# Seven tiles of one field's rows fetched by SyncE, and the first chunk numbers worked out on all partitions

## The chip, the cores and the metric

One core of a Trainium2 chip runs the kernel. The metric is the device time in microseconds. The kernel before took 483.76 us (median of three runs, 483.4 to 483.77).

## The reference

2048 samples have 13 dense features and 26 sparse fields. Each field has its own table of 12500 rows of 32 floats. The sparse numbers go up to 99998; a number past the end of its table reads the last row, and a negative one counts from the end, so the kernel clamps and wraps them.

```
emb = stack(table[f][sparse[:, f]])                  # 2048 x 26 x 32
bi  = emb[:, FIRST] * emb[:, SECOND]                 # 325 pairs of fields
a   = relu(bi @ att_w_w + att_w_b)                   # 32 -> 8
w   = softmax(a @ att_d_w + att_d_b over the pairs)
out = sigmoid(concat(sum(w * bi), dense) @ fin_w + fin_b)
```

## The kernel before, in words

The samples are 16 tiles of 128, taken in four blocks of four tiles (`QUADS`, the loop variable `q`). In a block the 26 fields are taken in order. For field `f`, `emb[:, f]` is a 128x128 tile: four tiles of samples (index `g` or `t = 4q + g`) with 32 numbers each.

How the rows get there depends on the field. For 23 fields GpSimd gathers them, one indirect DMA for each tile (line 368), so 92 in each block and 368 in all. It gathers a block's field as soon as VectorE has transposed the same field of the block before. For fields 3, 11 and 19 (`LOOK`) TensorE picks them: each table is in SBUF as 128 partitions x 7 chunks x 14 rows, VectorE makes one-hot columns from the chunk number of every sample (`make_onehots`, line 667, in two parts of 4 and 3 chunks), TensorE multiplies them with the table (`look_up`, line 391), and VectorE masks the right one of 14 rows and sums (lines 678, 681). This takes 12 tiles of two steps in each block, set between the other work by `STEP_FIELDS`. The steps of a block for field 3 stand in the block before; those of the first block stand at the very start, ahead of anything else on TensorE.

The chunk numbers go a long way. `look_index` comes in as 48x128, VectorE works out the chunk numbers on 48 partitions (lines 593 to 605), ACT's queue writes them to DRAM (`chunk_numbers`, line 495) and waits, and then reads the first block's back broadcast to all 128 partitions (line 498). SyncE does this for the later blocks into two buffers (`load_chunks`, line 337); for block `q` of 2 or more it first waits until the one-hots of block `q-2` are made. The same queue loads the three tables of 1568 KB (`load_table`, line 331): table 0 at once, table 1 after the first chunk numbers have landed, and table 2 after six transposes.

VectorE then transposes each field (lines 655, 657) and multiplies it with all fields before it into a ring of 8 groups of 16 pairs (line 691). TensorE multiplies each group with the attention weights (`first`, 405) and with the final weights (`sums_f`, 415), ACT applies the relu (507), TensorE sums the scores (429), and they go back transposed for the softmax. At the end of each block come maximum, exponentials and weighted sums (lines 717 to 772). Each engine's program is a fixed order written out by hand, joined by semaphores. SyncE has nothing to issue from its last `load_chunks` until it stores the result.

Of the kernel before, what the change touches and what calls it, by code (L numbers as in the profile page):

```python
# [5 lines left out]
P = 128  # L6
G = 4
# [8 lines left out]
HIDDEN = 6  # L16
BATCH = 4
LOOK = (3, 11, 19)
LOOK_TILES = (4, 4, 4)
CHUNKS = 7  # L20
CHUNK_ROWS = 14
# [16 lines left out]

def attention_fm(nc, dense, sparse, tables, params, look_index, chunk_numbers, out):
    f32, i32 = mybir.dt.float32, mybir.dt.int32  # L40
# [74 lines left out]
    def gathers_of(f):  # L115

        if f in LOOK:
            return G - LOOK_TILES[LOOK.index(f)]
        return G

# [47 lines left out]
    with ctx:  # L168
        def sb(name, shape, dt=f32):
            return ctx.enter_context(nc.sbuf_tensor(name, shape, dt))  # L170
# [4 lines left out]
        def sem(name):  # L175
# [6 lines left out]
        rows = sb("rows", [P, T, F], i32)  # L182
        emb = sb("emb", [P, F, G * D])

        look_table = sb("look_table", [P, LOOKS, CHUNKS, CHUNK_ROWS * D])

        index = sb("index", [QUADS * LOOKS * G, P], i32)
        index_clamped = sb("index_clamped", [QUADS * LOOKS * G, P])
        index_wrap = sb("index_wrap", [QUADS * LOOKS * G, P])
        index_part = sb("index_part", [QUADS * LOOKS * G, P])  # L190
        index_chunk = sb("index_chunk", [QUADS * LOOKS * G, P])
# [18 lines left out]
        wrap, moved = (weighed[:].rearrange("p g e -> p (g e)")[:, i * T * F:(i + 1) * T * F].rearrange(  # L210
            "p (t f) -> p t f", f=F) for i in range(2))
        neg_max = sb("neg_max", [P, G])
        neg_max_early = sb("neg_max_early", [P, G])
# [9 lines left out]
        feats = sb("feats", [P, T, N_DENSE])  # L223
        feats_w = sb("feats_w", [P, T, N_DENSE])
        linear = sb("linear", [P, T])
# [24 lines left out]
        rows_first_ready = sem("rows_first_ready")  # L250
        rows_ready = sem("rows_ready")
        gathered = [sem(f"gathered{f}") for f in range(F)]
        transposed = sem("transposed")
        look_table_in = [sem(f"look_table_in{n}") for n in range(len(LOOK))]
        index_in = sem("index_in")
        index_steps = sem("index_steps")
# [60 lines left out]

        def chunk_numbers_of(q):
            return chunk_numbers[q:q + 1].broadcast_to((P, LOOKS * G * P))

        block = ctx.enter_context(nc.Block())

        @block.sync
        def _(sp):
            sp.dma_start(ids[:], sparse.rearrange("(p t) f -> p t f", t=T)).then_inc(ids_in, 16)
            sp.dma_start(index[:], look_index).then_inc(index_in, 16)
            stacked = tables.rearrange("f v d -> (f v) d")

            def load_table(n):
                rows_n = stacked[LOOK[n] * V:LOOK[n] * V + P * PART_ROWS]  # L330
                sp.dma_start(look_table[:, n], rows_n.rearrange("(p c i) d -> p c (i d)", p=P, c=CHUNKS)
                             ).then_inc(look_table_in[n], 16)
# [8 lines left out]
            sp.dma_start(feats[:], dense.rearrange("(p t) n -> p t n", t=T)).then_inc(feats_in, 16)  # L341
# [12 lines left out]
        def _(pool):  # L354
            stacked = tables.rearrange("f v d -> (f v) d")
            pool.wait_ge(rows_first_ready, 1)
            for q in range(QUADS):
                for f in range(F):
                    if q == 0 and f == FIRST_FIELDS:
                        pool.wait_ge(rows_ready, 1)  # L360
                    if q and gathers_of(f):
                        pool.wait_ge(transposed, (q - 1) * F + f + 1)
                    for g in range(gathers_of(f)):
                        if q == 0 and f < FIRST_FIELDS:
                            row = rows_first[:, g, f:f + 1]
                        else:
                            row = rows[:, q * G + g, f:f + 1]
                        pool.indirect_dma_start(  # L368
                            emb[:, f, g * D:(g + 1) * D], None, stacked, bass.IndirectOffsetOnAxis(ap=row, axis=0),
                        ).then_inc(gathered[f], 16)  # L370

        @block.tensor
        def _(pe):
# [5 lines left out]
            for q in range(QUADS):  # L379

                def look_up(i):
                    of, n, g, part = steps[i]
                    pe.wait_ge(look_table_in[n], 16)
                    pe.wait_ge(onehot_made, (of * LOOKS + n) * len(STEPS) + part + 1)
# [104 lines left out]
        def _(act):  # L489
            act.dma_start(par[:, cols["offset"]], params[:, cols["offset"]]).then_inc(offsets_in, 16)  # L490
            rest = slice(cols["offset"].stop, params.shape[1])
            act.dma_start(par[:, rest], params[:, rest]).then_inc(par_in, 16)

            act.wait_ge(index_chunk_made, 1)
# [3 lines left out]
            act.dma_start(chunk_of[:, 0].rearrange("p n b -> p (n b)"), chunk_numbers_of(0)).then_inc(chunk_of_in[0], 16)  # L498
            act.wait_ge(par_in, 16)
            for q in range(QUADS):  # L500
# [71 lines left out]
        def _(dve):  # L572
# [4 lines left out]
            def make_rows(made, t, f, to, ready):  # L577
# [12 lines left out]


            dve.wait_ge(index_in, 16)
            nc.vector.tensor_scalar(index_clamped[:], index[:], float(-V), float(V - 1), ALU.max, ALU.min
# [19 lines left out]
            for n, f in enumerate(LOOK):  # L613
# [12 lines left out]
                                               look_id[:, n, :], ALU.mult, ALU.add).then_inc(look_id_steps, 1)  # L626
            dve.wait_ge(par_in, 16)
            dve.wait_ge(look_id_steps, 4 * LOOKS)
# [3 lines left out]
                                    ).then_inc(look_mask_made, 1)  # L632
            nc.vector.tensor_copy(chunk_here, par[:, cols["look_chunk"]]).then_inc(chunk_here_made, 1)
            dve.wait_ge(look_mask_made, 1)
            dve.wait_ge(chunk_here_made, 1)

# [8 lines left out]
            for q in range(QUADS):  # L645
# [14 lines left out]
                def make_onehots(of, n, part):  # L660
                    dve.wait_ge(chunk_of_in[of % 2], (of // 2 + 1) * 16)

                    if of or n:
                        dve.wait_ge(looked, first_step(of, n) - len(STEPS) + part + 1)
                    tiles, chunks = slice((G - LOOK_TILES[n]) * P, G * P), STEPS[part]
                    shape = (P, chunks.stop - chunks.start, LOOK_TILES[n] * P)
                    nc.vector.tensor_tensor(onehot[:, chunks, tiles],  # L667
                                            chunk_of[:, of % 2, n, tiles].unsqueeze(1).broadcast_to(shape),
                                            chunk_here[:, chunks].unsqueeze(2).broadcast_to(shape), ALU.is_equal
                                            ).then_inc(onehot_made, 1)  # L670

# [26 lines left out]
                if q == 0:  # L698
                    for i in steps_beside(q, 0):
                        for of, n, part in onehots_for([i]):  # L700
                            make_onehots(of, n, part)
                        for tile in tiles_ended([i - 1] if i else []):
                            take_looked(tile)
# [140 lines left out]
```

## Time and profile before

| | before |
|---|---|
| median of three runs | 483.76 us |
| the profiled execution's own time | 483.39 us |
| its span, first to last instruction | 481.6 us |
| PE busy / DVE busy / POOL busy / ACT busy | 450.2 / 372.6 / 347.9 / 95.8 us |
| mean granted TensorE clock | 0.996 |
| GpSimd's indirect DMAs | 368 |

The span is what the profile shows; the time has 1.8 us more around it. A busy share is an average over the whole span. Which engine sets the end of a stretch is read from the waits in that stretch.

### The profile page before, as it was taken

The numbers are of one execution on the slowest core, as the hardware profiler recorded it, in microseconds if no ns is written. First come the engines' busy times: TensorE is split into PE (matmuls) and PEld (weight loads), VectorE is DVE, ScalarE is ACT, GpSimd is POOL, SyncE is SP. The second block draws the span as 40 slices with busy tenths as digits, with TensorE's granted clock in tenths as the row PEclk, the third lists the DMA queues.
The fourth block names the chain that finished last, engine by engine and source line by source line (L and its number), as shares of the span: only waits on it lengthen the run. The fifth ranks groups of instructions, "written<-read, shape, count | busy, mean of one in ns | idle before, by whom it ended". The sixth has DMA issues, their size and how long they took to land.

```text
span 481.6 us, 6198 instructions
## 1 busy us (share of the span) xinstructions
PE 450.2 (93%) x2280; PEld 177.6 (37%) x2280; DVE 372.6 (77%) x645; ACT 95.8 (20%) x198; POOL 347.9 (72%) x372
## 2 busy tenths in 40 slices
PE   0699999999998999999999899999999899999884
PEld 0354443343333533333333443333334344333221
DVE  6337788796965979799775969879786788887985
ACT  0000101131252011112243101113234201114253
POOL 5777777777777777777777777777777777777740
PEclk9999999999999999999999999999999999999998
DMA  6933743121122223222112222213111222322210
GB/s 221 250 13 15 147 58 36 13 15 13 15 13 15 14 14 79 15 14 14 14 14 13 15 13 15 13 13 15 14 13 16 14 15 13 15 13 14 15 10 1
DMA packets 13661, 15.06 MB, mean 31 GB/s; under 512 B 6368, under 2 KB 12608, under 8 KB 13248
## 3 DMA queue, kind: packets, MB, share of 16 engines
q0 software_dynamic: 11776, 6.05, 23.1%
q1 hardware_dynamic: 1360, 7.53, 4.2%
q10 hardware_dynamic: 496, 1.09, 0.6%
q8 instruction: 18, 0.29, 0.2%
q14 instruction: 11, 0.09, 0.1%
HBM read 14.61 MB, written 0.03 MB: 30 GB/s over the span
## 4 chain that ended last, share of the span: by engine, by line
PE 78%; POOL 8%; DVE 5%; issue 4%; DMA 3%; ACT 1%; POOLq 0%; DVEq 0%
PE looked_own L391 33%; PE back_s L391 16%; PE first L405 13%; PE sums_f L415 12%; POOL emb L368 8%; PE sums_s L429 3%; DVE onehot L667 2%; DMA chunk_numbers<-index_chunk 1%; DMA emb<-tables,rows 1%; DMA chunk_of<-chunk_numbers 1%; PE back_f L442 1%; PE back_s L452 1%; DVE look_masked L678 1%; DMA par<-params 1%; DVE ring L691 0%
## 5 line engine op out<-in xcount | busy, mean ns | idle before, releaser
L368 POOL DMA_INDIRECT emb<-tables,rows x324 | 305.9, 944 | 98.7 <-issue 96.9
L691 DVE TENSOR_TENSOR ring<-emb_t,turned 128x512 f32<-128x512 f32 (+9 forms) x180 | 193.9, 1114 | 3.4
L391 PE MATMUL looked_own<-look_table,onehot 128*128 128x448 f32 x434 | 178.0, 554 | 17.0 <-DVE onehot L667 16.7
L391 PEld LDWEIGHTS looked_own<-look_table,onehot 128*128 128x128 f32 x434 | 79.5, 192 | 114.4 <-issue 114.4
L507 ACT ACTIVATE hidden<-first,par 128x512 f32<-128x512 f32 (+1 forms) x84 | 56.5, 678 | 284.7 <-PE first L405 284.4
L391 PE MATMUL back_s<-look_table,onehot 128*128 128x448 f32 x238 | 94.4, 545 | 3.1 <-DVE score L739 3.1
L405 PE MATMUL first<-ring,par 128*32 128x512 f32 (+1 forms) x672 | 90.7, 591 | 4.3 <-DVE ring L691 4.3
L415 PE MATMUL sums_f<-ring,par 128*32 128x512 f32 (+1 forms) x672 | 90.0, 583 | 0.0
L667 DVE TENSOR_TENSOR onehot<-chunk_of,turned 128x2048 f32<-128x2048 f32 (+1 forms) x24 | 48.3, 2018 | 26.6 <-PE looked_own L391 21.2
L391 PEld LDWEIGHTS back_s<-look_table,onehot 128*128 128x128 f32 x238 | 44.0, 190 | 51.7 <-issue 51.7
L368 POOL DMA_INDIRECT emb<-tables,rows_first x44 | 41.8, 950 | 17.2 <-issue 13.1
L678 DVE TENSOR_TENSOR look_masked<-looked_own,look_mask 128x448 f32<-128x448 f32 x31 | 19.3, 622 | 36.0 <-PE looked_own L391 36.0
L415 PEld LDWEIGHTS sums_f<-ring,par 128*32 128x32 f32 x672 | 22.8, 110 | 48.3 <-issue 47.4
L405 PEld LDWEIGHTS first<-ring,par 128*32 128x32 f32 x672 | 17.1, 108 | 57.5 <-issue 32.6
L655 DVE STREAM_TRANSPOSE turned<-emb 128x128 f32<-128x128 f32 x100 | 31.9, 319 | 1.9 <-DMA emb<-tables,rows 1.8
L681 DVE TENSOR_REDUCE emb<-look_masked 128x32 f32<-128x448 f32 x48 | 29.8, 620 | 1.6
L657 DVE STREAM_TRANSPOSE emb_t<-emb 128x128 f32<-128x128 f32 x100 | 27.1, 271 | 0.0
L429 PE MATMUL sums_s<-hidden,par 128*32 128x512 f32 (+1 forms) x168 | 25.1, 585 | 0.0
L678 DVE TENSOR_TENSOR look_masked<-back_s,look_mask 128x448 f32<-128x448 f32 x17 | 10.6, 621 | 15.7 <-PE back_s L391 15.7
L507 ACT ACT_TABLE_LOAD x1 | 1.3, 1283 | 57.9 <-PE first L405 57.9
L717 DVE TENSOR_REDUCE neg_max_early<-score 128x4 f32<-128x1024 f32 x4 | 4.9, 1217 | 8.8 <-ACT score L535 8.8
L520 ACT ACTIVATE second_s<-sums_s,par 128x512 f32<-128x512 f32 x12 | 8.3, 688 | 15.7 <-PE sums_s L429 15.7
(56 smaller groups left out, 101.0 us busy)
## 6 DMA issues: line engine op xcount, KB each, us to landing
emb<-tables,rows POOLq DMA_INDIRECT x324, 3.2
look_table<-tables SPq DMA_DIRECT2D x3, 1568.0 KB, 8.2
chunk_of<-chunk_numbers SPq DMA_DIRECT2D x3, 768.0 KB, 4.9
chunk_of<-chunk_numbers ACTq DMA_DIRECT2D x1, 768.0 KB, 3.8
emb<-tables,rows_first POOLq DMA_INDIRECT x44, 3.8
par<-params ACTq DMA_DIRECT2D x1, 258.5 KB, 3.1
ids<-sparse SPq DMA_DIRECT2D x1, 208.0 KB, 2.5
feats<-dense SPq DMA_DIRECT2D x1, 104.0 KB, 8.1
```

The lines of the kernel that those rows point to most:

```text
L368: pool.indirect_dma_start(emb[:, f, g * D:(g + 1) * D], None, stacked, bass.IndirectOffsetOnAxis(ap=row, axis=0),).then_inc(gathered[f], 16)
L391: mm = nc.tensor.matmul(looked_rows[look_bank[tile]], onehot[:, c, g * P:(g + 1) * P], look_table[:, n, c, :], start=c == 0, stop=c == CHU ...
L405: mm = nc.tensor.matmul(first[gr % 2][j * TILE:(j + 1) * TILE, 0:n * P], w, ring[:, gr % RING, 0:n, j, :], start=True, stop=True)
L415: mm = nc.tensor.matmul(sums_f[j * TILE:(j + 1) * TILE, 0:pairs_c(gr) * P], row, ring[:, gr % RING, 0:pairs_c(gr), j, :], start=e == 0, st ...
L429: mm = nc.tensor.matmul(sums_s[tile * TILE:(tile + 1) * TILE, cut], d_sel[:, half, :], hidden[:, gr % HIDDEN, cut], start=half == 0, stop= ...
L507: nc.scalar.activation(hidden[:, gr % HIDDEN, cut], first[gr % 2][:, cut], ACT.Relu, bias=par[:, cols["bias_a"]]).then_inc(relu_done, 1)
L655: tr = nc.vector.transpose(turned[:, f % 2, :], emb[:, f, :])
L657: tr = nc.vector.transpose(emb_t[:, f, :], emb[:, f, :])
L667: nc.vector.tensor_tensor(onehot[:, chunks, tiles], chunk_of[:, of % 2, n, tiles].unsqueeze(1).broadcast_to(shape), chunk_here[:, chunks]. ...
L678: nc.vector.tensor_tensor(look_masked[:], looked_rows[look_bank[tile]].rearrange("p (i d) -> p d i", d=D), mask, ALU.mult).then_inc(look_m ...
L681: nc.vector.tensor_reduce(emb[:, LOOK[n], g * D:(g + 1) * D], look_masked[:], AX.X, ALU.add).then_inc(look_summed, 1)
L691: nc.vector.tensor_tensor(slot[:, at:at + n, :], emb_t[:, i:i + n, :], turned[:, f % 2, :].unsqueeze(1).broadcast_to((P, n, P)), ALU.mult) ...
```

## The change

It has two parts.

**Field 21.** GpSimd no longer gathers tiles 2 and 3 of field 21 in each block (`PLACED` = 2, eight tiles). They land in a buffer of their own, `emb_placed`. One of the eight (tile 2 of the first block) GpSimd still gathers, now ahead of field 13 of the first block. The other seven (`TILES_SP` = 1, 2, 2, 2 for the four blocks) SyncE fetches row by row: it loads 32 row numbers from SBUF into registers and issues 32 DMAs of 128 bytes each, 896 in all. VectorE works out the numbers as 16x128 (`sp_ids`, three instructions, ahead of the dense features). The tiles of a block are copied into `emb` by one ACT instruction, which stands in ACT's order ahead of the relus of field 20 (`SP_PLACE`) and waits for them; VectorE's transpose of field 21 waits for this copy.

SyncE's other work moves with it. Table 1 is issued right behind table 0. After 32 rows of the first tile come table 2 and the chunk numbers of block 1; the chunk numbers of block 2 come after three tiles (384 rows), and those of block 3 after five tiles (640 rows).

**The first chunk numbers.** `look_index[0:4]` (field 3, first block) is brought broadcast to all 128 partitions (`index_first`, 128x512 int32) as SyncE's second DMA. VectorE works out its chunk numbers there in five instructions and makes the first one-hots from them, before the 48x128 chain; the second part of those one-hots comes right behind that chain, and the row numbers of all tiles after it. Table 0 is loaded in two DMAs, the chunks of each part by themselves. ACT's chunk read leaves field 3 out. `feats` moves from SyncE's queue to ACT's, and some scratch tiles now share memory with later ones.

```diff
 sync:
     sp.dma_start(ids[:], ...)
+    numbers_first = look_index[0:G].rearrange("(o g) p -> o (g p)", o=1)
+    sp.dma_start(index_first[:], numbers_first.broadcast_to((P, G * P))).then_inc(index_first_in, 16)
     sp.dma_start(index[:], look_index).then_inc(index_in, 16)
...
+                if n == 0:
+                    sp.dma_start(look_table[:, n, STEPS[0]], rows_n[:, STEPS[0]]).then_inc(look_table_first_in, 16)
+                    sp.dma_start(look_table[:, n, STEPS[1]], rows_n[:, STEPS[1]]).then_inc(look_table_in[n], 16)
...
     load_table(0)
-    sp.dma_start(feats[:], ...)
-    sp.wait_ge(chunk_of_in[0], 16)
+    sp.dma_start(sp_ids[:], sp_index).then_inc(sp_ids_in, 16)
     load_table(1)
-    load_chunks(1)
-    sp.wait_ge(transposed, 6)
-    load_table(2)
-    for q in range(2, QUADS):
-        load_chunks(q)
+    sp.wait_ge(sp_rows_ready, 1)
+    tiles = 0
+    for q in range(QUADS):
+        for i in range(PLACED - TILES_SP[q], PLACED):
+            t = q * G + G - PLACED + i
+            for p in range(0, P, ROWS_SP):
+                if tiles == 0 and p == P // 4:
+                    load_table(2)
+                    sp.wait_ge(chunk_numbers_home, 16)
+                    load_chunks(1)
+                _, at = nc.values_load_multi_w_load_instructions(
+                    sp_rows[t:t + 1, p:p + ROWS_SP], engines=(mybir.EngineType.SP,), min_val=0, ...)
+                for k in range(ROWS_SP):
+                    sp.dma_start(emb_placed[p + k:p + k + 1, q, i * D:(i + 1) * D],
+                                 stacked[bass.ds(at[k], 1), :]).then_inc(sp_gathered[tiles], 16)
+            tiles += 1
+        if 0 < q < QUADS - 1:
+            load_chunks(q + 1)
 gathers_of(f):
-        return G
+        return G - PLACED if f == SP_FIELD else G
 scalar:
+                def place_rows():
+                    act.wait_ge(placed_gathered, (QUADS * PLACED - sum(TILES_SP)) * 16)
+                    for i in range(sum(TILES_SP[:q]), sum(TILES_SP[:q + 1])):
+                        act.wait_ge(sp_gathered[i], P * 16)
+                    nc.scalar.activation(emb[:, SP_FIELD, PLACED_COLS], emb_placed[:, q, :], ACT.Copy
+                                         ).then_inc(placed, 1)
                 for f in range(1, F):
+                    if f == SP_PLACE:
+                        place_rows()
 vector:
+    # five instructions on index_first (128x512), as on index; the last writes chunk_of[:, 0, 0, :]
+    make_onehots(0, 0, 0)
     # the chain of lines 593 to 605 on index (48x128)
+    make_onehots(0, 0, 1)
     make_rows(3, T, F, rows, rows_ready)
...
+    # three instructions on sp_ids (16x128) -> sp_rows, sp_rows_ready
...
+                    if f == SP_FIELD:
+                        dve.wait_ge(placed, q + 1)
```

## Rows read from the trace of the kernel before

**Rows 1.** The page, busy time of each engine.
```profile
PE 450.2 (93%) x2280; PEld 177.6 (37%) x2280; DVE 372.6 (77%) x645; ACT 95.8 (20%) x198; POOL 347.9 (72%) x372
```

**Rows 2.** The chain that ended last, its last stretch: start us, us, what.
```profile
409.52 0.94 POOL emb L368
...
463.21 3.97 DMA emb<-tables,rows
```

**Rows 3.** The page's costliest groups: xcount | busy, mean ns | idle before, releaser.
```profile
L368 POOL DMA_INDIRECT emb<-tables,rows x324 | 305.9, 944 | 98.7 <-issue 96.9
```

**Rows 4.** The chain at the start, 0 to 50 us.
```profile
5.73 4.31 DMA chunk_numbers<-index_chunk
10.06 3.85 DMA chunk_of<-chunk_numbers
13.93 2.30 DVE onehot L667
16.36 7.71 PE looked_own L391 x14
...
41.87 1.75 DVE onehot L667
```

**Rows 5.** Timeline of DVE, last block: start us, us, what [idle before, releaser].
```profile
438.43 0.62 DVE L678 TENSOR_TENSOR look_masked<-looked_own,look_mask 128x448 f32<-128x448 f32 x1 [2.35 <-PE looked_own L391]
...
449.29 0.32 DVE L655 STREAM_TRANSPOSE turned<-emb 128x128 f32<-128x128 f32 x1
...
457.10 0.33 DVE L655 STREAM_TRANSPOSE turned<-emb 128x128 f32<-128x128 f32 x1 [0.66 <-DMA emb<-tables,rows]
...
461.76 0.33 DVE L655 STREAM_TRANSPOSE turned<-emb 128x128 f32<-128x128 f32 x1 [0.78 <-DMA emb<-tables,rows]
...
467.21 0.33 DVE L655 STREAM_TRANSPOSE turned<-emb 128x128 f32<-128x128 f32 x1 [0.36 <-DMA emb<-tables,rows]
```

**Rows 6.** Timeline of DVE at the start, 4 to 11 us.
```profile
4.10 0.21 DVE L586 TENSOR_TENSOR rows_first<-weighed 128x52 int32<-128x52 f32 x1
...
5.44 0.47 DVE L578 TENSOR_SCALAR clamped<-ids 128x416 f32<-128x416 int32 x1
...
5.95 0.44 DVE L581 TENSOR_SCALAR weighed<-clamped 128x416 f32<-128x416 f32 x1
...
6.31 0.58 DVE L584 TENSOR_TENSOR weighed<-clamped,par 128x416 f32<-128x416 f32 x1
...
10.10 0.86 DVE L631 TENSOR_TENSOR look_mask<-par,look_i 128x672 f32<-128x672 f32 x1
```

**Rows 7.** DMA issues: KB each, median us from issue to landing.
```profile
look_table<-tables SPq DMA_DIRECT2D x3, 1568.0 KB, 8.2
chunk_of<-chunk_numbers SPq DMA_DIRECT2D x3, 768.0 KB, 4.9
...
index<-look_index SPq DMA_DIRECT2D x1, 24.0 KB, 2.7
```

**Rows 8.** Timeline of SyncE's queue, DMA issues.
```profile
1.18 0.42 SPq L326 DMA_DIRECT2D index<-look_index  x1
1.65 0.41 SPq L331 DMA_DIRECT2D look_table<-tables  x1
...
49.14 0.33 SPq L331 DMA_DIRECT2D look_table<-tables  x1
```

**Rows 9.** Timeline of DVE, one-hots of field 3 for blocks 2 and 3, first parts.
```profile
207.54 2.29 DVE L667 TENSOR_TENSOR onehot<-chunk_of,turned 128x2048 f32<-128x2048 f32 x1 [1.05 <-PE looked_own L391]
...
320.87 2.29 DVE L667 TENSOR_TENSOR onehot<-chunk_of,turned 128x2048 f32<-128x2048 f32 x1 [1.05 <-PE looked_own L391]
```

**Rows 10.** Timeline of ACT, relu of the group that completes field 19.
```profile
115.60 0.69 ACT L507 ACTIVATE hidden<-first,par 128x512 f32<-128x512 f32 x1 [4.37 <-PE first L405]
...
446.62 0.69 ACT L507 ACTIVATE hidden<-first,par 128x512 f32<-128x512 f32 x1 [1.03 <-PE first L405]
```

**Rows 11.** Timeline of DVE in the first block, behind field 21's products.
```profile
120.59 0.62 DVE L678 TENSOR_TENSOR look_masked<-looked_own,look_mask 128x448 f32<-128x448 f32 x1 [2.94 <-PE looked_own L391]
```

More of the change, by code:

```diff
@@ L17 @@
 BATCH = 4
+ROWS_SP = 32
+SP_FIELD = 21
+TILES_SP = (1, 2, 2, 2)
+PLACED = 2
+SP_PLACE = 20
+SP_FIRST = 13
 LOOK = (3, 11, 19)
@@ L118, in gathers_of @@
             return G - LOOK_TILES[LOOK.index(f)]
-        return G
+        return G - PLACED if f == SP_FIELD else G
+    PLACED_COLS = slice((G - PLACED) * D, G * D)
+    assert FIRST_FIELDS <= SP_FIRST < SP_PLACE < SP_FIELD and len(TILES_SP) == QUADS and max(TILES_SP) <= PLACED
+    assert SP_FIELD not in LOOK
     assert G * D == P and B % (P * G) == 0 and RING < GROUPS and 1 < END_GROUPS
@@ L211, in attention_fm @@
             "p (t f) -> p t f", f=F) for i in range(2))
+        index_first = final[:].rearrange("p g e -> p (g e)")[:, 0:G * P].bitcast(i32)
+        index_clamped, index_wrap, index_part = (
+            final[0:QUADS * LOOKS * G].rearrange("p g e -> p (g e)")[:, G * P + i * P:G * P + (i + 1) * P] for i in range(3))
+        first_clamped, first_part = (score[:].rearrange("p g e -> p (g e)")[:, i * G * P:(i + 1) * G * P] for i in range(2))
+        sp_clamped, sp_wrap = (weighed[0:T].rearrange("p g e -> p (g e)")[:, i * P:(i + 1) * P] for i in range(2))
         neg_max = sb("neg_max", [P, G])
@@ L251, in attention_fm @@
         rows_ready = sem("rows_ready")
+        sp_ids_in = sem("sp_ids_in")
+        sp_steps = sem("sp_steps")
+        sp_rows_ready = sem("sp_rows_ready")
+        sp_gathered = [sem(f"sp_gathered{i}") for i in range(sum(TILES_SP))]
+        placed_gathered = sem("placed_gathered")
+        placed = sem("placed")
         gathered = [sem(f"gathered{f}") for f in range(F)]
@@ L360, in _ @@
                         pool.wait_ge(rows_ready, 1)
+                    if q == 0 and f == SP_FIRST:
+                        for n in range(QUADS):
+                            for i in range(PLACED - TILES_SP[n]):
+                                t = n * G + G - PLACED + i
+                                pool.indirect_dma_start(
+                                    emb_placed[:, n, i * D:(i + 1) * D], None, stacked,
+                                    bass.IndirectOffsetOnAxis(ap=rows[:, t, SP_FIELD:SP_FIELD + 1], axis=0),
+                                ).then_inc(placed_gathered, 16)
                     if q and gathers_of(f):
@@ L382, in look_up @@
                     of, n, g, part = steps[i]
-                    pe.wait_ge(look_table_in[n], 16)
+                    pe.wait_ge(look_table_first_in if n == 0 and part == 0 else look_table_in[n], 16)
                     pe.wait_ge(onehot_made, (of * LOOKS + n) * len(STEPS) + part + 1)
@@ L492, in _ @@
             act.dma_start(par[:, rest], params[:, rest]).then_inc(par_in, 16)
+            act.dma_start(feats[:], dense.rearrange("(p t) n -> p t n", t=T)).then_inc(feats_in, 16)
             act.wait_ge(index_chunk_made, 1)
@@ L588, in _, with make_onehots @@
             make_rows(0, G, FIRST_FIELDS, rows_first, rows_first_ready)
+            dve.wait_ge(index_first_in, 16)
+            nc.vector.tensor_scalar(first_clamped, index_first[:], float(-V), float(V - 1), ALU.max, ALU.min
+                                    ).then_inc(index_first_steps, 1)
+            dve.wait_ge(index_first_steps, 1)
+            nc.vector.tensor_scalar(first_part, first_clamped, 0.0, float(V), ALU.is_lt, ALU.mult
+                                    ).then_inc(index_first_steps, 1)
+            dve.wait_ge(index_first_steps, 2)
+            nc.vector.scalar_tensor_tensor(first_part, first_clamped, -0.5 * (CHUNK_ROWS - 1), first_part,
+                                           ALU.add, ALU.add).then_inc(index_first_steps, 1)
+            dve.wait_ge(index_first_steps, 3)
+            nc.vector.tensor_scalar(first_clamped, first_part, 1.0 / CHUNK_ROWS, 2.0 ** 23, ALU.mult, ALU.add
+                                    ).then_inc(index_first_steps, 1)
+            dve.wait_ge(par_in, 16)
+            nc.vector.tensor_copy(chunk_here, par[:, cols["look_chunk"]]).then_inc(chunk_here_made, 1)
+            dve.wait_ge(index_first_steps, 4)
+            nc.vector.tensor_scalar(chunk_of[:, 0, 0, :], first_clamped, -2.0 ** 23, None, ALU.add
+                                    ).then_inc(chunk_first_made, 1)
+            def make_onehots(of, n, part):
+                if of == 0 and n == 0:
+                    dve.wait_ge(chunk_first_made, 1)
+                    dve.wait_ge(chunk_here_made, 1)
+                else:
+                    dve.wait_ge(chunk_of_in[of % 2], (of // 2 + 1) * 16)
+                    dve.wait_ge(looked, first_step(of, n) - len(STEPS) + part + 1)
+                tiles, chunks = slice((G - LOOK_TILES[n]) * P, G * P), STEPS[part]
+                shape = (P, chunks.stop - chunks.start, LOOK_TILES[n] * P)
+                nc.vector.tensor_tensor(onehot[:, chunks, tiles],
+                                        chunk_of[:, of % 2, n, tiles].unsqueeze(1).broadcast_to(shape),
+                                        chunk_here[:, chunks].unsqueeze(2).broadcast_to(shape), ALU.is_equal
+                                        ).then_inc(onehot_made, 1)
+            make_onehots(0, 0, 0)
             dve.wait_ge(index_in, 16)
@@ L632, in _ @@
                                     ).then_inc(look_mask_made, 1)
-            nc.vector.tensor_copy(chunk_here, par[:, cols["look_chunk"]]).then_inc(chunk_here_made, 1)
             dve.wait_ge(look_mask_made, 1)
-            dve.wait_ge(chunk_here_made, 1)
+            dve.wait_ge(sp_ids_in, 16)
+            nc.vector.tensor_scalar(sp_clamped[:], sp_ids[:], float(-V), float(V - 1), ALU.max, ALU.min
+                                    ).then_inc(sp_steps, 1)
+            dve.wait_ge(sp_steps, 1)
+            nc.vector.tensor_scalar(sp_wrap[:], sp_clamped[:], 0.0, float(V), ALU.is_lt, ALU.mult).then_inc(sp_steps, 1)
+            dve.wait_ge(sp_steps, 2)
+            nc.vector.scalar_tensor_tensor(sp_rows[:], sp_clamped[:], float(SP_FIELD * V), sp_wrap[:], ALU.add, ALU.add
+                                           ).then_inc(sp_rows_ready, 1)
             dve.wait_ge(feats_in, 16)
@@ L658, in turn_field @@
                     tr.then_inc(transposed, 1)
[L660 to L670, printed above, removed]
                 def take_looked(tile):
```

35 lines of the change are left out of this document (20 added, 15 removed).

## The prediction

> **What bounds the kernel now.** I read four views in this order: busy times, the chain that ended last, the waits of each engine, and the timelines of both ends.
>
> The busy times say that TensorE has work for 450.2 us of the 481.6 us span [rows 1]. So 31 us are idle, and the question is where. The timelines put 16.4 us of it ahead of the first matmul and most of the rest in the last 30 us.
>
> The chain names GpSimd as the end: from 409.52 to 463.21 it holds only gathers, then one gather's landing of 3.97 us [rows 2]. GpSimd gathers without a pause: one takes 0.944 us, and the 0.30 us between two are its own issue time, not a wait [rows 3]. So a gather costs 1.25 us, and 368 of them fill 4.6 to 464 us. But a chain shows one string of work only. VectorE, in its tail, waits for TensorE's last look-up until 438.43 and is then busy to the end but for three waits for gathers: 0.66, 0.78 and 0.36 us, 1.80 us in all [rows 5]. That is all that faster gathers alone could give. Take more away and VectorE is the limit, and what sets when its tail begins is TensorE, which reached 438 us with the work of four blocks behind it and hardly a gap since 16.36.
>
> What holds TensorE until 16.36 is a string of transfers: 4.31 us for the chunk numbers to DRAM, 3.85 us back to all partitions, 2.30 us for the one-hots [rows 4]. So the two parts of the change go together: one moves GpSimd's limit, the other TensorE's and VectorE's.
>
> **The first chunk numbers.** The term is the new start of TensorE.
> 1. `index_first` is issued second on SyncE's queue, at 1.18 [rows 8]. The 24 KB in that place landed after 2.7 us, at 3.9; a table's 1568 KB took 8.2 us [rows 7], so 1544 KB more cost 5.5 us, 281 KB a microsecond. The 256 KB broadcast adds 0.9 us: landed at 4.8. VectorE is free at 4.31 [rows 6] and waits for it.
> 2. Five instructions on 128x512. At 416 elements an integer one starts 0.51 us ahead of the next, a float one takes 0.44 and about 0.03 to the next, one with two operands 0.58 [rows 6]. Times 512/416: 0.63 + 0.58 + 0.75 + 0.58 + 0.58 = 3.1 us, and 0.2 us for the small copy of `chunk_here` in between. Done at 8.1.
> 3. First one-hots 2.30 us [rows 4]: done at 10.4, first matmul 0.13 us later at 10.5, against 16.36. The gain is 5.9 us.
>
> Bounds: if `index_first` costs nothing beyond 4.31 and 512 elements no more than 416, the start is 9.3 (gain 7.1). If it moves at the rate of the 768 KB chunk read, 4.9 us for all of it [rows 7], and table 0 is late too, about 11.5 (gain 4.9). Table 0 as a whole would land at 1.65 + 8.2 + 0.9 = 10.8, and its first part, four chunks of seven, is needed at 10.5; it should be in by 9.
>
> The second one-hots come behind the 48x128 chain (1.4 us, from 4.31 to 5.73) and take 1.75 [rows 4]: done at 13.6. TensorE's first step is 8 of the 14 matmuls that took 7.71 us [rows 4], so it ends after 14.9. That is covered by 1.3 us.
>
> What moves behind them: the row numbers, look ids and mask took from 5.44 to 10.96 [rows 6] and now end at 19.1, the three 16x128 instructions at 19.8, and the dense features (1.1 us, beside TensorE) at 20.9. VectorE must mask tile 0 before TensorE wants that bank for tile 2, at about 10.5 + 7.7 + 5.3 = 23.5. Covered by 2 us; without that cover each microsecond goes onto the start. GpSimd needs the later row numbers only after 44 gathers, past 55 us. The other chunk numbers of block 0 are now written at 11.8 and should be home by about 20 with their two transfers, beside table 1; the one-hots of field 11 want them 5.9 us ahead of 37.7, so 12 us cover them.
>
> From 10.5 us on TensorE does the same matmuls in the same order. Its gaps between one-hots (near 40 and 43 us) and at block ends hang on its own results and shift along. I expect the 5.9 us to arrive whole at 438.
>
> **The gathers.** Seven fewer are 7 x 1.25 = 8.7 us off GpSimd's end. The eighth tile is only moved, ahead of field 13 in block 0, where gathers are many microseconds early. At the end VectorE asks 5.9 us sooner and gathers land 8.7 us sooner, 2.8 us more margin than before: for fields 23 and 24 waits of 0.66 and 0.78 vanish, and at field 25 VectorE arrives 5.9 + 0.66 + 0.78 + 0.36 = 7.7 us sooner than it started before, still after the landing (8.7). The next thing late is VectorE itself.
>
> **Field 21's wait.** VectorE's transpose of field 21 waits for ACT's copy, and the copy stands behind the relu that completes field 19. In block 0 that relu ended at 116.29 [rows 10] where VectorE started field 21 at 114.1, so VectorE stops for some 2.7 us. Behind the transpose its products wait, and then it idled 2.94 us for a look-up until 120.59 anyway [rows 11]. The stop fills that idle time and costs nothing; blocks 1 and 2 repeat the pattern. In block 3 the relu ended at 447.31 [rows 10] and VectorE came at 449.29 [rows 5]: 1.3 us are left after a copy of 0.35 us. ACT's later relus wait behind that copy too, 0.35 us beside TensorE's two-bank lead.
>
> **SyncE.** This is the unknown. SyncE starts at 19.8 us. The cost of a row is one DMA issue and its share of a register load. No row of the trace shows a DMA with an address from a register. Issues last 0.33 us alone and 0.41 to 0.42 us in a row, and two stand 0.47 us apart [rows 8]. So a row costs between 0.33 and 0.50 us: the top is 0.47 and the 0.03 us that the trace shows between dependent instructions. I take 0.43, nearest to the issues that follow each other. By the shift of 5.9 us the deadlines are:
> - chunk numbers of block 3, behind 640 rows: wanted at 320.87 - 5.9 = 315.0 [rows 9], landing 4.9 us [rows 7]. (315.0 - 4.9 - 19.8) / 640 = 0.454 us a row.
> - chunk numbers of block 2, behind 384 rows: (207.54 - 5.9 - 4.9 - 19.8) / 384 = 0.461.
> - the last tile, 896 rows: ACT is free for it at 447.31 - 5.9 = 441.4, less 3 us of landing: 418.6 / 896 = 0.467.
> - the first tile: 0.68.
>
> At 0.43 us the chunk numbers of block 3 land at 300, 15 us early, and the last row is issued at 405. The tightest condition isn't the rows but the chunk read queued behind them.
>
> The Trainium skill speaks against this part in one place: in DMA: Bandwidth & Descriptors, Latency and other measured facts, it gives a floor of about 600 ns for a `tensor_load`. No row here shows one. By it 28 loads of 32 numbers would add 17 us to SyncE's path, 0.019 us a row; 0.43 becomes 0.449, still just below 0.454, and the sum would be the same.
>
> **The sum**, against the profiled execution: span 481.6 - 5.9 - 1.8 = 473.9; its own time 483.39 - 7.7 = 475.7. The median of the runs shown is 0.37 above that execution, so 476.1 us.
>
> **Rivals.**
> A. *SyncE is too slow* (slower). Above 0.454 us a row the chunk numbers of block 3 come late, and VectorE's one-hots, with all its later products behind them, wait. Each 0.01 us costs 6.4 us. The gain of 7.7 is gone at 0.466. At 0.47 the time is 476.1 + 10.4 = 486.5; at 0.50 it is 476.1 + 29.6 = 505.7. For it: the spacing of 0.47 in [rows 8], and the unseen register work. Against it: 0.33 to 0.42 as durations, and a single 128-byte row has less to describe than 128 partitions. If the number loads cost as much as the issue again (0.86 us a row), block 3's numbers land at 575 and the time is near 736; I give that 2 in 100 within A.
> B. *Part of the start is lost.* `index_first`, table 0 and both `par` loads share the first microseconds, or VectorE is late for tile 0's mask. With 3 us of gain instead of 5.9: 479.0. For it: margins of 1.3 to 2 us. Against: a shift of all of them is already in the 4.9 of the bounds.
> C. *The start gives nothing*, because of a wait that I don't see, and only the waits for gathers go: 483.8 - 1.8 = 482.0.
> D. *GpSimd still binds.* If the start gains 7.1, GpSimd's 8.7 is the limit: 483.8 - 8.7 = 475.1. This is the low end of the forecast.
> E. *No change*, a late chunk read that eats just the gain (0.464 to 0.468 us a row): 482.8 to 484.7.
>
> **How the numbers follow.** Forecast with D 0.62, B 0.08, C 0.04, E 0.04, A 0.22. Faster is 0.74, same 0.04, slower 0.22; 0.2%, about 1 us, is what a measurement of this kernel tells from no change. The forecast's own range is 474.6 to 477.2, from gains at the start of 7.1 (stopped by GpSimd at 8.7) to 4.9. For 8 in 10 the range has to reach into A: 474.4 to 488, where the top is a row cost of 0.473.
>
> **What would show it.** The first matmul at 9.3 to 11.5 us. SyncE's issues 0.40 to 0.45 us apart, its last row before 425 us, block 3's chunk read well before 310. No wait of VectorE for gathers at fields 23 to 25. Its last look-up mask near 432.5 instead of 438.4. ACT's copy in block 3 without a wait for SyncE. Wrong would be: one-hots of block 2 or 3 that wait for `chunk_of`, ACT idle ahead of the copy of field 21 for a DMA, or a first matmul early and a mask of tile 0 that TensorE waits for.

## The result, and the profile after

The changed kernel takes 501.02 us (median of four runs, 499.64 to 502.38) against 483.76 (four runs, 483.4 to 483.82) for the kernel before: a ratio of 1.0359, 95% interval 1.0337 to 1.0381. The forecast was 476.1 us, with 488 as the top of its range. Rival A happened: SyncE is too slow. The profile is of the slowest of the four runs: time 502.38 us, span 500.6 us.

The page of the changed kernel, busy times, the granted clock in 40 slices of 12.5 us, and the chain by engine and line:

```profile
PE 454.6 (91%) x2280; PEld 179.5 (36%) x2280; DVE 375.7 (75%) x653; ACT 96.4 (19%) x202; POOL 341.4 (68%) x365
...
PEclk9999999999999999959999999995999999999998
...
SPq 46%; PE 24%; issue 17%; DVE 9%; DMA 2%; ACT 1%
SPq L391 37%; PE looked_own L446 9%; SPq L387 9%; PE back_s L446 4%; PE first L460 4%; DVE ring L791 4%; PE sums_f L470 4%; PE sums_s L484 1%; DVE onehot L686 1%; DMA chunk_of<-chunk_numbers 1%; DMA final<-look_index 1%; DVE turned L767 0%; DVE look_masked L778 0%; PE back_f L497 0%; PE back_s L507 0%
```

GpSimd is gone from the chain and SyncE's queue (SPq) holds 46% of the span: line 391 is the row DMA, line 387 the register load. TensorE's 2280 matmuls are busy 4.4 us longer than in [rows 1], and two slices show a clock near half.

The queue of SyncE, timeline: start us, us, what.

```profile
22.99 13.47 SPq L391 DMA_DIRECT2D emb_placed<-tables  x32
36.50 0.37 SPq L365 DMA_DIRECT2D look_table<-tables  x1
36.91 0.43 SPq L370 DMA_DIRECT2D chunk_of<-chunk_numbers  x1
...
208.18 0.36 SPq L370 DMA_DIRECT2D chunk_of<-chunk_numbers  x1
210.85 122.18 SPq L391 DMA_DIRECT2D emb_placed<-tables  x256
333.08 0.36 SPq L370 DMA_DIRECT2D chunk_of<-chunk_numbers  x1
335.76 122.10 SPq L391 DMA_DIRECT2D emb_placed<-tables  x256
```

From one chunk read to the next, 333.08 - 208.18 = 124.9 us pass for 256 rows: 0.488 us a row. The 32 rows behind one load take 13.47 us, 0.42 each; the rest is the loads, 2.16 us for 32 numbers or 0.067 us a row. The instructions of the two lines (duration in ns min/median/max, first and last start us):

```profile
L387 SPq TENSOR_LOAD <-sp_rows x28: 2032/2158/2290, 20.7 to 442.3; - x28
...
L391 SPq FUSED_REGOPS  x896: 37/37/46, 22.8 to 457.5; - x180
L391 SPq MOVE emb_placed<-tables x896: 29/29/29, 22.9 to 457.6; - x180
L391 SPq DMA_DIRECT2D emb_placed<-tables x896: 224/225/303, 23.0 to 457.6; - x180
```

What this does to VectorE, timeline of DVE, the one-hots of field 3 for blocks 2 and 3 (before: [rows 9]) and the field 21 transposes that wait for ACT's copy:

```profile
213.43 2.29 DVE L686 TENSOR_TENSOR onehot<-chunk_of,turned 128x2048 f32<-128x2048 f32 x1 [11.69 <-DMA chunk_of<-chunk_numbers]
...
237.89 0.33 DVE L767 STREAM_TRANSPOSE turned<-emb 128x128 f32<-128x128 f32 x1 [2.35 <-ACT emb L606]
...
339.33 2.29 DVE L686 TENSOR_TENSOR onehot<-chunk_of,turned 128x2048 f32<-128x2048 f32 x1 [11.49 <-DMA chunk_of<-chunk_numbers]
```

Two waits for chunk reads, 23.2 us together. The read issued at 333.08 landed at 339.33, 6.2 us later. Behind the wait TensorE starts slowly. Timeline of PE, and a row of the windows view (stretch, its length, busy us and instructions of PE, PEld, DVE, ACT and POOL, granted clock, DMA share, GB/s):

```profile
325.51 3.27 PE L446 MATMUL looked_own<-look_table,onehot 128*128 128x448 f32 x8
...
345.24 5.69 PE L446 MATMUL looked_own<-look_table,onehot 128*128 128x448 f32 x8 [10.29 <-DVE look_masked L778]
...
345.00:350.00 5.00, 4.76 (x7) 2.34 (x8) 4.93 (x7) 0.00 (x0) 3.78 (x5) 0.50 0.15 17
```

The same eight matmuls take 5.69 us after 10.3 us of idling and 3.27 before it. The granted clock is 0.50 from 345 to 350 us, the lower of the two levels (1.2 GHz instead of 2.4); from 325 to 335 us, before the stop, it is 1.00.

And the start, timelines of DVE and PE (before: [rows 4], [rows 6]):

```profile
3.98 0.21 DVE L652 TENSOR_TENSOR rows_first<-weighed 128x52 int32<-128x52 f32 x1
6.76 0.43 DVE L659 TENSOR_SCALAR score<-final 128x512 f32<-128x512 int32 x1 [2.56 <-DMA final<-look_index]
...
9.58 2.29 DVE L686 TENSOR_TENSOR onehot<-chunk_of,turned 128x2048 f32<-128x2048 f32 x1
...
12.02 7.31 PE L446 MATMUL looked_own<-look_table,onehot 128*128 128x448 f32 x14 [12.02 <-DVE onehot L686]
```

`index_first` (its memory is `final`) landed at 6.74. The chain from there to the one-hots took 2.8 us, and the first matmul came at 12.0 instead of 16.4.

### The profile page after: what moved, and what is told of

Read it like the earlier page. It is cut to its first block, busy times and chain, and to the rows that moved or that the text cites. A ratio compares the mean times of both kernels' runs of the same rounds, so it can differ in the third digit from the quotient of the medians.

```text
span 500.6 us, 8933 instructions
## 1 busy us (share of the span) xinstructions
PE 454.6 (91%) x2280; PEld 179.5 (36%) x2280; DVE 375.7 (75%) x653; ACT 96.4 (19%) x202; POOL 341.4 (68%) x365
## 4 chain that ended last, share of the span: by engine, by line
SPq 46%; PE 24%; issue 17%; DVE 9%; DMA 2%; ACT 1%
SPq L391 37%; PE looked_own L446 9%; SPq L387 9%; PE back_s L446 4%; PE first L460 4%; DVE ring L791 4%; PE sums_f L470 4%; PE sums_s L484 1%; DVE onehot L686 1%; DMA chunk_of<-chunk_numbers 1%; DMA final<-look_index 1%; DVE turned L767 0%; DVE look_masked L778 0%; PE back_f L497 0%; PE back_s L507 0%
## 5 line engine op out<-in xcount | busy, mean ns | idle before, releaser
L423 POOL DMA_INDIRECT emb<-tables,rows x316 | 298.4, 944 | 96.4 <-issue 94.9
L446 PE MATMUL looked_own<-look_table,onehot 128*128 128x448 f32 x434 | 182.3, 565 | 33.4 <-DVE look_masked L778 20.8
L446 PEld LDWEIGHTS looked_own<-look_table,onehot 128*128 128x128 f32 x434 | 81.4, 196 | 133.3 <-issue 133.3
L686 DVE TENSOR_TENSOR onehot<-chunk_of,turned 128x2048 f32<-128x2048 f32 (+1 forms) x24 | 48.4, 2017 | 46.0 <-DMA chunk_of<-chunk_numbers 23.2
L470 PEld LDWEIGHTS sums_f<-ring,par 128*32 128x32 f32 x672 | 22.8, 110 | 48.3 <-issue 47.4
L484 PE MATMUL sums_s<-hidden,par 128*32 128x512 f32 (+1 forms) x168 | 25.1, 585 | 0.0
L778 DVE TENSOR_TENSOR look_masked<-back_s,look_mask 128x448 f32<-128x448 f32 x17 | 10.6, 622 | 13.5 <-PE back_s L446 13.5
## 6 DMA issues: line engine op xcount, KB each, us to landing
look_table<-tables SPq DMA_DIRECT2D x2, 1568.0 KB, 10.3
```

Of the source, the lines that this page charges most:

```text
L423: pool.indirect_dma_start(emb[:, f, g * D:(g + 1) * D], None, stacked, bass.IndirectOffsetOnAxis(ap=row, axis=0),).then_inc(gathered[f], 16)
L446: mm = nc.tensor.matmul(looked_rows[look_bank[tile]], onehot[:, c, g * P:(g + 1) * P], look_table[:, n, c, :], start=c == 0, stop=c == CHU ...
L470: mm = nc.tensor.matmul(sums_f[j * TILE:(j + 1) * TILE, 0:pairs_c(gr) * P], row, ring[:, gr % RING, 0:pairs_c(gr), j, :], start=e == 0, st ...
L484: mm = nc.tensor.matmul(sums_s[tile * TILE:(tile + 1) * TILE, cut], d_sel[:, half, :], hidden[:, gr % HIDDEN, cut], start=half == 0, stop= ...
L686: nc.vector.tensor_tensor(onehot[:, chunks, tiles], chunk_of[:, of % 2, n, tiles].unsqueeze(1).broadcast_to(shape), chunk_here[:, chunks]. ...
L778: nc.vector.tensor_tensor(look_masked[:], looked_rows[look_bank[tile]].rearrange("p (i d) -> p d i", d=D), mask, ALU.mult).then_inc(look_m ...
```

## The experiments

My theory was that all parts work but one: the register loads lift a row from 0.42 to 0.49 us and so over 0.454 us, where the chunk read of block 3 comes late. The main rival was that 896 small DMAs hurt in themselves. Each ratio is against runs of the kernel before on the same chip.

**one_load.** The edit:

```diff
+                        if tiles == 0 and p == 0:
                             _, at = nc.values_load_multi_w_load_instructions(...)
```

> Only the first 32 row numbers are loaded into registers; all 896 row DMAs use these 32 registers again, so 27 of 28 register loads are left out and most rows brought are the wrong ones. Theory 1 (the register loads, 2.16 us for 32 numbers, lift a row from 0.42 to 0.49 us and so over the 0.454 us at which the chunk numbers of block 3 come late): a row costs 0.42 us, block 3's chunk read is issued near 290 instead of 333 us, no one-hots wait for it, and the time is 483.8 - 4.3 (start) - 1.8 (gathers) = 477.6 us. Theory 2 (the 896 small DMAs themselves are what hurts, through the queue, the DMA engines or ACT's copy): time stays within 3 us of the changed kernel's 501 us.

Measured: 477.1 us, ratio 0.9868 (0.9851 to 0.9884). If the numbers are spread evenly up to 99998, seven of eight in this field are clamped to the table's last row, so fewer rows differ than was written. All 896 DMAs are still issued, so their number does no harm. The queue of this kernel:

```profile
22.95 13.48 SPq L392 DMA_DIRECT2D emb_placed<-tables  x32
...
37.41 115.86 SPq L392 DMA_DIRECT2D emb_placed<-tables  x352
...
238.23 84.10 SPq L392 DMA_DIRECT2D emb_placed<-tables  x256
```

The time came out as forecast, but the rate did not. The first 32 rows take 0.42 us each as before and the later ones 0.33 us, where 0.42 was expected for all. So this run leaves out more than the loads. The rows of line 392 show what:

```profile
L392 SPq MOVE emb_placed<-tables x896: 29/29/29, 22.9 to 322.0; - x180
L392 SPq DMA_DIRECT2D emb_placed<-tables x896: 224/228/470, 22.9 to 322.1; - x180
L392 SPq FUSED_REGOPS  x32: 37/37/46, 22.8 to 36.1; - x32
```

Only 32 of the 896 rows have the arithmetic that makes an address of a row number (FUSED_REGOPS); I take it that the address of a number used before is kept. The instruction lasts 0.037 us, but the rows that have it stand 0.09 us further apart.

**six_tiles.** The edit is one line: `TILES_SP = (1, 1, 2, 2)`.

> SyncE fetches one tile in block 1 instead of two (1, 1, 2, 2: six tiles, 768 rows); GpSimd gathers the other early. Theory 1: the chunk numbers of block 2 then stand behind 256 rows (issued near 148 us, wanted near 203) and those of block 3 behind 512 rows (near 272, wanted near 316.5), the last row is issued near 397 us; no wait for SyncE is left, GpSimd is 7.5 us shorter, and the time is 477.6 us. Theory 2 (any large number of row DMAs costs time in proportion): 18 us of loss times 6/7 leaves about 498 us.

Measured: 476.73 us, ratio 0.9855 (0.9838 to 0.9871). The chunk reads were issued at 146.7 and 271.5. Theory 1. The end of this kernel, timeline of DVE (before: [rows 5]):

```profile
434.12 0.62 DVE L778 TENSOR_TENSOR look_masked<-looked_own,look_mask 128x448 f32<-128x448 f32 x1 [2.36 <-PE looked_own L446]
...
452.04 0.32 DVE L767 STREAM_TRANSPOSE turned<-emb 128x128 f32<-128x128 f32 x1
...
455.84 0.32 DVE L767 STREAM_TRANSPOSE turned<-emb 128x128 f32<-128x128 f32 x1
...
461.04 0.32 DVE L767 STREAM_TRANSPOSE turned<-emb 128x128 f32<-128x128 f32 x1
```

VectorE's tail begins 4.3 us sooner, and the waits for gathers at fields 23 to 25 are gone. 4.3 + 1.8 = 6.1 us, and the span is 475.5 against 481.6.

At the start not all of the earlier first matmul is kept. Timelines of PE, six_tiles and then the kernel before (its first matmul: [rows 4]):

```profile
11.67 8.11 PE L446 MATMUL looked_own<-look_table,onehot 128*128 128x448 f32 x14 [11.67 <-DVE onehot L686]
19.62 5.42 PE L446 MATMUL back_s<-look_table,onehot 128*128 128x448 f32 x14
...
23.91 2.42 PE L391 MATMUL back_s<-look_table,onehot 128*128 128x448 f32 x6
```

The first matmul is 4.7 us earlier, the second tile's first one 4.3 us.

This kernel also tells where the changed kernel's time went. The one-hots of field 3 for block 3, six_tiles, and the last look-up mask of the changed kernel, timelines of DVE:

```profile
316.56 2.29 DVE L686 TENSOR_TENSOR onehot<-chunk_of,turned 128x2048 f32<-128x2048 f32 x1 [1.05 <-PE looked_own L446]
...
459.23 0.62 DVE L778 TENSOR_TENSOR look_masked<-looked_own,look_mask 128x448 f32<-128x448 f32 x1 [2.35 <-PE looked_own L446]
```

The one-hots are 339.33 - 316.56 = 22.8 us later in the changed kernel. The last mask is 459.23 - 434.12 = 25.1 us later, and so is the end (500.6 - 475.5). The 2.3 us between are near the 2.4 us that the eight matmuls behind the second stop took longer.

**start_alone.** SyncE fetches no rows, GpSimd gathers all of field 21, and ACT's copy and its wait are gone. Table 2 waits for six transposes again, and the chunk reads of blocks 2 and 3 stand behind no rows. The start is the changed kernel's.

```diff
-        return G - PLACED if f == SP_FIELD else G
+        return G
```

> The start of the changed kernel alone: first chunk numbers worked out on all partitions, table 0 in two parts, but GpSimd gathers all 368 tiles and SyncE fetches no rows. Theory 1 (two limits side by side): TensorE starts at 12.0 us, but GpSimd's gathers still end at 464, VectorE's waits for gathers at fields 23 to 25 grow from 1.8 to about 6 us, and the time is that of before, 483.8 us, within 0.5. Rival (the start is the limit, and GpSimd only looks like one): 479.5 us.

Measured: 484.17 us, ratio 1.0011 (1.0001 to 1.002). TensorE starts at 11.7, and it is worth nothing (0.1% slower, an interval that only just leaves out 1). The waits of its DVE (us in total, times, longest):

```profile
DVE turned L742 <- DMA emb<-tables,rows: 12.9, 11, 2.0
```

Before, this was 1.8 us in three waits. The forecast of the time held, that of the place did not: at fields 23 to 25 the waits stay at 2.0 us (1.58 and 0.45), where about 6 were expected, and the rest stand at other fields. Time won at the start is handed back to the gathers piece by piece.

**chunks_on_act.** Seven tiles; the chunk reads leave SyncE's queue.

```diff
+                if 0 < q < QUADS - 1:      # ACT, at the start of block q
+                    act.wait_ge(onehot_made, q * (LOOKS * len(STEPS)))
+                    act.dma_start(chunk_of[:, (q + 1) % 2]..., chunk_numbers_of(q + 1)).then_inc(chunk_of_in[(q + 1) % 2], 16)
```

> Seven tiles as in the changed kernel, but the chunk reads of blocks 2 and 3 are issued by ACT's queue at the start of blocks 1 and 2 instead of behind SyncE's rows. Theory 1: the one-hots wait no more, but now the last tile's rows decide: the last row is issued near 457 us and lands near 459.5, VectorE wants field 21 at 445, so it loses about 15 us there: 492.5 us. If the chunk reads were the only thing late, the time would be 477.6 us; if they were not the cause, 501 us.

Measured: 491.24 us, ratio 1.0151 (1.0134 to 1.0168). The second deadline is real, at the place that was named. Timelines of ACT and DVE:

```profile
458.64 0.26 ACT L608 ACTIVATE emb<-emb_placed 128x64 f32<-128x64 f32 x1 [15.46 <-DMA emb_placed<-tables]
...
459.00 0.33 DVE L769 STREAM_TRANSPOSE turned<-emb 128x128 f32<-128x128 f32 x1 [13.76 <-ACT emb L608]
```

**byte_offsets.** Seven tiles where the change has them. One more small VectorE instruction makes byte offsets, and the DMA takes them without arithmetic.

```diff
+            nc.vector.tensor_scalar(sp_rows[:], sp_clamped[:], float(4 * D), None, ALU.mult).then_inc(sp_rows_ready, 1)
...
-                                         stacked[bass.ds(at[k], 1), :])
+                                         tables.rearrange("f v d -> (f v d)").bitcast(mybir.dt.uint8)[bass.ds(at[k], 4 * D)]...)
```

> The changed kernel with all seven tiles in their places, but VectorE works out byte offsets (one more 16x128 instruction, times 128) and the row DMAs take them as they are, so the register arithmetic ahead of each row DMA is gone; the 28 register loads stay. With one load in all and no arithmetic behind the first 32 rows, rows were 0.33 us apart. If the arithmetic costs 0.09 us and the load 0.067 us a row, a row costs 0.40 us, block 3's chunk read is issued near 277 us, the last row near 380, and the time is 476.7 us. If a row costs 0.42 us or more however its address is made, it is issued near 303 and the time is 476.7 us too, with the spacing telling; at 0.49 us as in the changed kernel, 501 us.

Measured: 477.17 us, ratio 0.9866 (0.985 to 0.9883). From chunk read to chunk read 277.76 - 175.29 = 102.5 us pass for 256 rows, 0.400 us a row with the loads still there:

```profile
175.29 0.36 SPq L370 DMA_DIRECT2D chunk_of<-chunk_numbers  x1
177.90 99.81 SPq L391 DMA_DIRECT2D emb_placed<-tables  x256
277.76 0.36 SPq L370 DMA_DIRECT2D chunk_of<-chunk_numbers  x1
```

So the same work in the same order is 1.3% faster than before or 3.6% slower, by 0.09 us of register arithmetic a row. All 896 rows are the right ones here, so the rival is out for them too. The loads alone were not taken away; by these numbers a row would then cost 0.42 us, which is also under 0.454. So it took the arithmetic and the loads together to make the chunk reads late.

**load16.** `ROWS_SP = 16`.

> The changed kernel with 16 row numbers in a register load instead of 32, so 56 loads instead of 28. If a load costs by the number, 0.067 us each, a load takes 1.08 us and the time stays near 501 us. If 2.16 us is the cost of a load whatever it brings, 40 loads ahead of block 3's chunk read instead of 20 put it 43 us later and the time is near 545 us.

Measured: 509.03 us, one run. A load of 16 numbers lasts 1.25 us, of 32 numbers 2.16:

```profile
L387 SPq TENSOR_LOAD <-sp_rows x56: 1160/1247/1423, 20.8 to 461.4; - x56
```

A straight line through these two sizes gives 0.057 us a number and 0.34 us beside it. It was nearly the first case. The 40 short loads ahead of block 3's read take 6.7 us more than 20 long ones, and the read is issued at 341.1 instead of 333.1; the other 1.3 us are not in the durations of the loads.

**six_old_start.** Six tiles with the start of the kernel before.

```diff
-            sp.dma_start(index_first[:], ...)      # and its five instructions, and table 0 in two parts
+            sp.wait_ge(chunk_of_in[0], 16)         # ahead of table 1 again
...
-            act.dma_start(chunk_of[:, 0, 1:]..., chunk_numbers_of(0, 1))
+            act.dma_start(chunk_of[:, 0]..., chunk_numbers_of(0))
```

> Six tiles fetched by SyncE (1, 1, 2, 2) with the start of the kernel before: chunk numbers only by way of DRAM, table 0 in one DMA, TensorE from 16.4 us. Theory 1 (two limits): GpSimd's gathers end 7.5 us sooner, only VectorE's 1.8 us of waits for gathers vanish, 481.6 to 482.2 us. Rival (GpSimd is the limit by itself): 476.3 us.

Measured: 483.5 us, but from 481.25 to 486.3 over ten runs, ratio 1.0005 (0.9982 to 1.0027). The median is above the 481.6 to 482.2 of theory 1; the profiled execution, 481.25, fits it, and the rival's 476.3 is out. The spread asked for another look:

> The same kernel as six_old_start, whose executions lay between 481.3 and 486.3 us. If this profile is one of the longer ones, it shows where: gathers or one-hots that land late in one of the blocks, or a lower granted clock. If it is a short one, 481.3 us again, nothing is learned.

That execution took 486.28 us. The chains of the two at the start, first the one of 481.25:

```profile
5.63 4.47 DMA chunk_numbers<-index_chunk
10.12 4.10 DMA chunk_of<-chunk_numbers
14.32 2.30 DVE onehot L659
16.75 5.50 PE looked_own L441 x10
```

and the one of 486.28:

```profile
5.63 6.07 DMA chunk_numbers<-index_chunk
11.72 6.12 DMA chunk_of<-chunk_numbers
17.93 2.30 DVE onehot L659
20.37 1.83 PE looked_own L441 x2
```

The same two transfers took 8.6 us in one and 12.2 in the other, and the first matmul is 3.6 us later; the span is 5.1 us longer. Of the other 1.5 us, 1.4 are the first tile's 14 matmuls, which took 8.43 us instead of 7.00. The row DMAs are not under way yet at 5 to 18 us, so they aren't the reason. What was changed in these microseconds is `feats` on ACT's queue ahead of the chunk numbers, and `sp_ids`. Which of them it is was not tried.

**six_numbers_act and combined.** Two tries for a better start.

```diff
 # six_numbers_act: six tiles; on ACT's queue, ahead of the bulk of params
+            act.dma_start(index_first[:], numbers_first.broadcast_to((P, G * P))).then_inc(index_first_in, 16)
 # combined: seven tiles with byte_offsets, the line above, and look_chunk brought with the first small transfer
+            early_cols = slice(0, cols["look_chunk"].stop)
+            act.dma_start(par[:, early_cols], params[:, early_cols]).then_inc(offsets_in, 16)
```

> Six tiles, and index_first is brought by ACT's queue ahead of the bulk of params instead of by SyncE's behind ids. In the changed kernel it landed 5.5 us after its issue, where 3.6 were predicted. If its place behind ids on one queue is the reason, it lands by 5.5 us, the first matmul comes near 10.6 and the time is 475.7 us. If all the transfers of the first microseconds share one rate, it lands at 6.3 to 6.8 again and the time is that of six_tiles, 476.7 us.

> Seven tiles with byte offsets, index_first on ACT's queue ahead of the bulk of params, and the chunk columns that chunk_here copies brought with the first small transfer, so that the copy no longer waits for the bulk. In six_numbers_act index_first landed 0.9 us sooner, but that copy then waited 1.5 us for params. If that wait was all that ate the gain, the first matmul comes near 10.9 us instead of 11.7 and the time is 476.2 us; if table 0's first part is late now, first matmul and time stay as in six_tiles, 476.7 us.

> The same kernel as six_tiles, on the same chip as combined: 476.7 us.

Measured: six_numbers_act 477.32 us (0.9859 to 0.9892); combined 477.22 (0.9844 to 0.9877) beside six_tiles_again 477.37 (0.9848 to 0.9881). Neither brought its forecast of 475.7 and 476.2 us. In the first, `index_first` landed at 5.9, but the small copy then waited for `params` until 9.5 and the first matmul came at 12.46, where 10.6 was hoped for. In the second this wait is gone, and the first matmul came at 11.39 (forecast 10.9) against 12.05 in six_tiles_again. But the first tile's 14 matmuls in combined:

```profile
11.39 8.53 PE L444 MATMUL looked_own<-look_table,onehot 128*128 128x448 f32 x14 [11.39 <-DVE onehot L686]
19.75 5.42 PE L444 MATMUL back_s<-look_table,onehot 128*128 128x448 f32 x14
```

The first 14 take 8.5 us and the next 14 take 5.4. Over the kernels with the new start this first tile took 7.0 to 8.5 us: combined, with the earliest first matmul, reached its second tile at 19.75, and six_numbers_act, with the latest, at 19.30. In six_tiles single matmuls of this first tile lasted from 0.54 to 1.09 us, with a granted clock of 1.00 from 10 to 25 us. Why is not shown, and a few tenths of a microsecond won here can't be told from no change. None of the four faster versions is shown to beat another; all lie 6.4 to 6.9 us under the kernel before.

## Why the prediction was wrong

*What bounds the kernel.* Right. Two limits lie side by side: start_alone moves one and gets nothing, six_old_start moves the other and gets 2.2 us of span in its shortest execution (nothing by its median, 483.5), six_tiles moves both and gets 6.9. One reading was too short: VectorE's tail has four more waits, 2.7 us in all, for TensorE and ACT at the very end. They are the same 2.7 us in six_tiles, so the sum does not hang on them.

*The first chunk numbers.* Right in kind, 1.5 us too good. `index_first` landed 5.5 us after its issue instead of 3.6; the arithmetic took 2.8 us instead of 3.3. The first matmul at 12.0 lies outside the bounds of 9.3 to 11.5, and the gain was 4.3 us instead of 5.9; in this much rival B happened too. The transfer was priced at a table's mean rate. Why it took longer is not shown; issued by ACT's queue ahead of `params` it landed after 4.7 us.

*The shift.* Right: the 4.3 us that six_tiles has left when its first tile is done arrive whole at the last look-up (434.12 against 438.43). That the first tile would take longer than before, 8.1 us instead of 7.7, was not foreseen.

*The gathers.* Right. 1.8 us, and then VectorE is the limit.

*Field 21's wait.* Right. VectorE stops 2.3 us in each of blocks 0 to 2, 7.0 us in all, and six_tiles has the same 7.0 us of stops and loses nothing by them.

*SyncE.* **This step failed.** "I take 0.43 us, nearest to the issues that follow each other." A row costs 0.488 us: 0.33 for the issue with its MOVE, 0.09 for the address arithmetic (0.42 against 0.33 in one_load), and 0.067 for its share of a register load (2.16 us / 32). The plain issue was priced too high and the register work, for which no row stood, at nothing. The sum lay just inside the bound of 0.50, and a threshold at 0.454 lay between the value that I took and that bound. The rest of the step held: the deadline of block 3's chunk read decides, block 2's is next (VectorE waits nearly the same for both, 11.7 and 11.5 us, because block 3's deadline is itself moved by the first wait), and the last tile's rows come third, as chunks_on_act shows at 491.2.

The floor of 600 ns for a `tensor_load` in the Trainium skill (DMA: Bandwidth & Descriptors, Latency and other measured facts) is not contradicted: no load here took less than 1.16 us. By that floor 28 loads would cost an estimated 17 us; they cost 28 x 2.16 = 60 us, and load16 shows that the size of a load counts.

*The price of rival A.* By its own rule, 0.488 us a row gives 476.1 + 0.034 x 640 = 497.9 us. Measured 501.0. The rule foresaw block 3's chunk read landing at 337.0 against a deadline of 315.0, 22.0 us late. It landed at 339.3 against 316.6 in six_tiles, 22.8 us late: it was issued 1.0 us later and took 6.2 us to land instead of 4.9, and the deadline was later because the start gained less. The rule had no term for the 2.3 us that TensorE loses at the lower clock behind the stop, and its base of 476.1 us was 0.6 to 1.3 us too low (the kernels without a wait take 476.7 to 477.4).

*The chance.* The threshold (0.454 for the first loss, 0.466 for the whole gain) lay well inside the bounds of the unknown cost (0.33 to 0.50). Spread evenly over these bounds the chance is 0.27 above the one and 0.20 above the other, so 0.22 fits them. It was too little because the top bound was itself made of rows that had no register instruction in them.

*The range.* Its low end of 474.6 us does not come out of the terms: D, which is called the low end, gives 475.1. Nothing measured hangs on it.

## What to carry to other kernels

An idle engine isn't a free one: give its work a rate, list every deadline of what is queued behind it, and compare the rate with the tightest, which here was a 768 KB read behind the rows and not the rows. Where a loop runs hundreds of times, price each instruction of its body, the loads and arithmetic of registers too; if no trace shows them, the unknown is wide and one changed size (six tiles for seven) that moves the deadlines out of its bounds is worth more than the last tile. When two limits lie side by side, either half of the change alone is worth little (start_alone nothing, the other half 2.2 us in its best execution), so judge such halves together.

## What the hardware showed that I had not expected

- A register load costs by the number: 2.16 us for 32, 1.25 us for 16.
- A DMA issue to one row lasts 0.225 us, where those to 128 partitions lasted 0.33 to 0.42 [rows 8], and back to back they stand 0.33 us apart; a register instruction of 0.037 us between two of them makes it 0.42.
- The 768 KB chunk reads of blocks 2 and 3 took 5.2 and 6.2 us to land in the changed kernel, 4.9 before [rows 7], but 4.1 and 4.3 in byte_offsets, where they also stand among row DMAs. What sets this is not shown.
- After 10.3 us of idling TensorE's next eight matmuls took 5.69 us instead of 3.27; the granted clock was 0.50 from 345 to 350 us, so TensorE ran at the lower of its two levels there, 1.2 GHz instead of 2.4. Two stops of that kind come with a mean clock of 0.976 instead of 0.996.
